# Down projection of a cross-attention and quantised FFN layer: a ring of four residual buffers in place of two, and two staging tiles

## The reference

```python
def _act_fake_quant(x, clip_factor):
    scale = jax.nn.sigmoid(clip_factor) * jnp.max(jnp.abs(x)) / QMAX
    return jnp.clip(_ste_round(x / scale), -QMAX - 1.0, QMAX) * scale
...
x = x + attention(layernorm(x), ctx)          # below: x1
xq = _act_fake_quant(layernorm(x), clip_x[0])
gate = xq @ quant(w_gate).T                   # 512 -> 1408
up = xq @ quant(w_up).T
h = _act_fake_quant(silu(gate) * up, clip_down[0])
x = x + h @ quant(w_down).T                   # 1408 -> 512
```

## Time and profile before

| | us |
|---|---|
| runs shown (3), median | 1185.84 (1184.47 to 1187.43) |
| the profiled execution, its time | 1187.88 |
| its span, first to last instruction | 1186.0 |
| PE busy | 1106.8 (93%) |
| DVE busy | 802.1 (68%) |
| ACT busy | 619.7 (52%) |
| POOL busy | 401.5 (34%) |

### The profile page before, as it was taken

The page is one execution under the profiler, slowest core; times in us unless marked ns, Lnnn a source line. Parts: engine busy times, 40 slices in busy tenths (PEclk is TensorE's granted clock), DMA queues, the critical chain, the costliest instruction groups (busy, mean ns, idle before and its releaser), DMA issues. The chain is left out here.

```text
span 1186.0 us, 17468 instructions
## 1 busy us (share of the span) xinstructions
PE 1106.8 (93%) x6173; PEld 625.7 (53%) x6202; DVE 802.1 (68%) x1478; ACT 619.7 (52%) x757; POOL 401.5 (34%) x317
## 2 busy tenths in 40 slices
PE   5988999999999999999999969999999999699898
PEld 4645555655666666666665534444444444244333
DVE  5455667677766776766655567787777777566565
ACT  3346555454555555554544436657566664754450
POOL 5454444355353644343321200000000000357578
PEclk8979999999999999999999979999999999799999
DMA  6234556556454545443215626766767512799977
GB/s 238 69 89 110 157 149 160 150 160 152 146 152 143 166 129 164 130 142 104 75 54 161 223 75 230 250 223 234 241 220 253 171 52 89 320 413 418 422 298 261
DMA packets 138736, 219.23 MB, mean 185 GB/s; under 512 B 59040, under 2 KB 67872, under 8 KB 132768
## 3 DMA queue, kind: packets, MB, share of 16 engines
q1 hardware_dynamic: 138656, 218.19, 56.3%
HBM read 133.48 MB, written 72.48 MB: 174 GB/s over the span
## 5 line engine op out<-in xcount | busy, mean ns | idle before, releaser
L1038 POOL TENSOR_TENSOR c_y<-x,c_y 128x512 f32<-128x512 f32 x64 | 112.7, 1794 | 395.2 <-DVE c_y L1072 380.5
L690 PE MATMUL a_Q<-a_xT,wq 128*128 128x512 f32 x768 | 199.8, 410 | 19.0 <-POOL a_xT L425 16.8
L690 PEld LDWEIGHTS a_Q<-a_xT,wq 128*128 128x128 f32 x768 | 144.2, 194 | 73.4 <-issue 22.6
L960 PE MATMUL e_G<-e_cT,gu 128*128 128x512 bf16 x689 | 180.0, 381 | 2.3 <-ACT e_cT L883 1.5
L924 DVE SCALAR_TENSOR_TENSOR h<-e_U,x_gus,e_sg 128x512 f32<-128x512 f32 x176 | 131.8, 749 | 73.2 <-PE e_U L964 47.4
L869 ACT ACTIVATE e_sg<-e_G,x_gus 128x512 f32<-128x512 f32 x176 | 119.0, 685 | 117.6 <-PE e_G L960 117.6
L964 PE MATMUL e_U<-e_cT,gu 128*128 128x512 bf16 x690 | 179.7, 381 | 0.7
L735 PE MATMUL a_O<-a_wo,a_aT 128*128 128x512 f32 x720 | 176.8, 395 | 0.0
L1110 PE MATMUL c_Y<-dn,gu 128*128 128x512 bf16 x704 | 156.8, 386 | 13.5 <-DVE gu L1065 13.5
L501 ACT ACTIVATE a_qT<-a_q 128x512 fp32r<-128x512 f32 x64 | 40.4, 631 | 216.9 <-DVE a_q L599 216.9
L735 PEld LDWEIGHTS a_O<-a_wo,a_aT 128*128 128x128 f32 x720 | 133.4, 189 | 28.0 <-issue 2.5
(11 more groups left out here) (128 smaller groups left out, 1351.0 us busy)
## 6 DMA issues: line engine op xcount, KB each, us to landing
x<-x_d SPq DMA_DIRECT2D x32, 1024.0 KB, 7.4
h_d<-h SPq DMA_DIRECT2D x24, 1024.0 KB, 4.1
h<-h_d SPq DMA_DIRECT2D x11, 1536.0 KB, 17.2
a_xr<-in_x SPq DMA_DIRECT2D x64, 256.0 KB, 2.9
a_xt<-in_xT SPq DMA_DIRECT2D x64, 256.0 KB, 3.1
x_d<-a_xr SPq DMA_DIRECT2D x64, 256.0 KB, 2.0
a_xs<-in_x SPq DMA_DIRECT2D x60, 256.0 KB, 2.9
out<-c_y SPq DMA_DIRECT2D x15, 1024.0 KB, 9.7
```

Of the source, the lines that this page charges most:

```text
L690: mm = nc.tensor.matmul(Q[:], wq[:, wp, j, P * n.g:P * (n.g + 1)], xT[:, n.par, xp, j], start=(ins == 0), stop=(ins == 3 * KT - 1))
L960: mm = nc.tensor.matmul(G[:, t % GU], gu[:, t, k], cT[:, p, k], start=(k == 0), stop=(k == KT - 1))
L1038: nc.gpsimd.tensor_tensor(y[:, p, t], x1[:, p, t], y[:, p, t], ALU.add).then_inc(added, 1)
```

## The change

`contract` alone is edited.

- **x1 buffers.** The store buffer of before (2 x 4 tiles) becomes `z` and joins `x1` in a ring of four block buffers, `ring(k)`. POOL adds the scaled tile into the residual in place (L1059), and the output is stored from the ring (L1034). SP loads the x1 of blocks 2 and 3 at the very start (L1021), and of block k+1 in turn k (from 3 on), after a wait for the store of block k-3, whose buffer it takes.
- **Staging.** `y` has only two tiles. The scaling of tile i waits until POOL has added tile i-2.
- **First block.** Its 11 inner tiles are coded and cast in pieces of 1, 1, 2, 2, 2 and 3 (`FIRST_CH`); PE takes its 44 matmuls inner tile by inner tile, over four PSUM banks, as the pieces come (L1120).
- **Later blocks.** PE waits for each of the two chunks only where it reads it (L1130). All loops are written out.
- **Last block.** DVE, not POOL, adds its residual (L1093), tile by tile after the scaling.
- **The scale.** The copy to `tall` is gone; the transpose reads `tmax` broadcast, and a `memset` of one column carries the signal.

```diff
--- before.py
+++ after.py
@@ -987,61 +987,76 @@
         dns = sb("h_dns", [P, D])
         c8 = sb("c_c8", [P, 2, IT, TOK], I8)
         cb = gu[:].rearrange("p t k n -> p (t k n)").rearrange("p (b t n) -> p b t n", b=2, t=IT)
-        tall = sb("h_tall", [P, P])
-        y = sb("c_y", [P, 2, TT, D])
+        z = sb("c_z", [P, 2, TT, D])
+        y = sb("c_y", [P, 2, D])
         Y = ps("c_Y", [P, 2 * TT, D])
         s_tmax, s_gmax, s_hinv, s_own = (sem("h_" + n) for n in ("tmax", "gmax", "hinv", "own"))
         h_in = [[sem(f"c_h_in{n}{b}") for b in range(NH)] for n in range(2)]
-        x1_in = [sem(f"c_x1_in{p}") for p in range(2)]
-        y_out = [sem(f"c_y_out{p}") for p in range(2)]
-        coded, cast, downed, scaled, added = (sem("c_" + n) for n in ("coded", "cast", "downed", "scaled", "added"))
+        x1_in = [sem(f"c_x1_in{r}") for r in range(4)]
+        y_out = [sem(f"c_y_out{r}") for r in range(4)]
+        last_out = sem("c_last_out")
+        coded, cast, downed, scaled, added, last_added = (sem("c_" + n) for n in (
+            "coded", "cast", "downed", "scaled", "added", "last_added"))
         CH = ((0, 6), (6, IT))
-        LAST = BLOCKS // 2
+        FIRST_CH = ((0, 1), (1, 2), (2, 4), (4, 6), (6, 8), (8, IT))
+        LAST = BLOCKS - 1
+
+        def pieces(k):
+
+            return FIRST_CH if k == 0 else CH
+
+        def upto(k, tile):
+
+            return sum(len(pieces(b)) for b in range(k)) + sum(hi <= tile for _, hi in pieces(k))
+
+        def ring(k):
+
+            return x1[:, k % 4] if k % 4 < 2 else z[:, k % 4 - 2]
 
         with nc.Block() as block:
 
             @block.sync
             def _(sp):
                 def load_x1(k):
-                    sp.dma_start(x1[:, k % 2], x1_d[ORDER[k]].rearrange("t p d -> p t d")).then_inc(x1_in[k % 2], 16)
-
-                for k in range(BLOCKS + 2):
+                    sp.dma_start(ring(k), x1_d[ORDER[k]].rearrange("t p d -> p t d")).then_inc(x1_in[k % 4], 16)
+
+                load_x1(2)
+                load_x1(3)
+                for k in range(BLOCKS + 1):
                     if k < BLOCKS - NH:
 
-                        for n, (a, z) in enumerate(CH):
-                            sp.wait_ge(coded, k * len(CH) + n + 1)
-                            sp.dma_start(h[:, BUFFER[k], a:z].rearrange("p t n -> p (t n)"),
-                                         h_d[ORDER[k + NH], :, TOK * a:TOK * z]).then_inc(h_in[n][k % NH], 16)
+                        for n, (a, e) in enumerate(CH):
+                            sp.wait_ge(coded, upto(k, e))
+                            sp.dma_start(h[:, BUFFER[k], a:e].rearrange("p t n -> p (t n)"),
+                                         h_d[ORDER[k + NH], :, TOK * a:TOK * e]).then_inc(h_in[n][k % NH], 16)
                     if k >= 2:
-
-                        if k - 2 < BLOCKS - 1:
-                            sp.wait_ge(added, (k - 1) * TT)
-                        if k - 2 < BLOCKS - 1:
-                            sp.dma_start(out_t[ORDER[k - 2]].rearrange("t p d -> p t d"), y[:, k % 2]).then_inc(y_out[k % 2], 16)
-                        if k < BLOCKS:
-                            load_x1(k)
+                        sp.wait_ge(added, (k - 1) * TT)
+                        sp.dma_start(out_t[ORDER[k - 2]].rearrange("t p d -> p t d"), ring(k - 2)).then_inc(y_out[(k - 2) % 4], 16)
+                    if 3 <= k < LAST:
+
+                        sp.wait_ge(y_out[(k - 3) % 4], 16 * ((k - 3) // 4 + 1))
+                        load_x1(k + 1)
 
                 for t in range(TT):
-                    sp.wait_ge(added, (BLOCKS - 1) * TT + t + 1)
-                    sp.dma_start(out_t[ORDER[BLOCKS - 1], t], y[:, 1, t]).then_inc(y_out[1], 16)
-                sp.wait_ge(y_out[0], 16 * LAST)
-                sp.wait_ge(y_out[1], 16 * (LAST - 1 + TT))
+                    sp.wait_ge(last_added, t + 1)
+                    sp.dma_start(out_t[ORDER[LAST], t], ring(LAST)[:, t]).then_inc(last_out, 16)
+                for r in range(4):
+                    sp.wait_ge(y_out[r], 16 * len(range(r, LAST, 4)))
+                sp.wait_ge(last_out, 16 * TT)
+
+            def residual_in(eng, k):
+
+                if k >= 2:
+                    eng.wait_ge(x1_in[k % 4], 16 * (k // 4 + (k % 4 >= 2)))
 
             @block.gpsimd
             def _(pool):
-                def add(u, p):
-                    k = 2 * u + p
-                    if not isinstance(u, int) or u > 0:
-                        pool.wait_ge(x1_in[p], 16 * u)
+                for k in range(LAST):
+                    residual_in(pool, k)
                     for t in range(TT):
-                        pool.wait_ge(scaled, k * TT + t + 1)
-                        nc.gpsimd.tensor_tensor(y[:, p, t], x1[:, p, t], y[:, p, t], ALU.add).then_inc(added, 1)
-
-                add(0, 0)
-                add(0, 1)
-                with pool.Fori(1, LAST) as u:
-                    for p in range(2):
-                        add(u, p)
+                        i = k * TT + t
+                        pool.wait_ge(scaled, i + 1)
+                        nc.gpsimd.tensor_tensor(ring(k)[:, t], ring(k)[:, t], y[:, i % 2], ALU.add).then_inc(added, 1)
 
             @block.scalar
             def _(act):
@@ -1049,73 +1064,72 @@
                 for k in range(BLOCKS):
 
                     if k >= 2:
-                        act.wait_ge(cast, (k - 1) * len(CH))
-                    for n, (lo, hi) in enumerate(CH):
+                        act.wait_ge(cast, upto(k - 2, IT))
+                    for lo, hi in pieces(k):
                         if k >= NH:
-                            act.wait_ge(h_in[n][k % NH], 16 * (k // NH))
+                            act.wait_ge(h_in[CH.index((lo, hi))][k % NH], 16 * (k // NH))
                         nc.scalar.activation(c8[:, k % 2, lo:hi], h[:, BUFFER[k], lo:hi], ACT.Copy, scale=hinv[:, 0:1]).then_inc(coded, 1)
 
             @block.vector
             def _(dve):
-                def to_bf16(u, p):
-                    k = 2 * u + p
+                own = Chain(dve, s_own)
+
+                def to_bf16(k):
                     after(dve, downed, (k - 1) * TT, 1 << 30)
-                    for n, (lo, hi) in enumerate(CH):
-                        dve.wait_ge(coded, k * len(CH) + n + 1)
-                        nc.vector.tensor_copy(cb[:, p, lo:hi], c8[:, p, lo:hi]).then_inc(cast, 1)
-
-                def scale(u, p):
-                    k = 2 * u + p
-                    after(dve, y_out[p], 16 * u, 1 << 30)
+                    for lo, hi in pieces(k):
+                        dve.wait_ge(coded, upto(k, hi))
+                        nc.vector.tensor_copy(cb[:, k % 2, lo:hi], c8[:, k % 2, lo:hi]).then_inc(cast, 1)
+
+                def scale(k):
                     for t in range(TT):
-                        dve.wait_ge(downed, k * TT + t + 1)
-                        nc.vector.tensor_tensor(y[:, p, t], Y[:, TT * p + t], dns[:], ALU.mult).then_inc(scaled, 1)
-
-                own = Chain(dve, s_own)
+                        i = k * TT + t
+                        after(dve, added, min(i - 1, LAST * TT), 1 << 30)
+                        dve.wait_ge(downed, i + 1)
+                        nc.vector.tensor_tensor(y[:, i % 2], Y[:, TT * (k % 2) + t], dns[:], ALU.mult).then_inc(scaled, 1)
+                        if k == LAST:
+                            dve.wait_ge(scaled, i + 1)
+                            if t == 0:
+                                residual_in(dve, k)
+                            nc.vector.tensor_tensor(ring(k)[:, t], ring(k)[:, t], y[:, i % 2], ALU.add).then_inc(last_added, 1)
+                            dve.wait_ge(last_added, t + 1)
+
                 own.step(nc.vector.tensor_reduce(tmax[:], hmax[:], AX.X, ALU.max))
-                nc.vector.tensor_copy(tall[:], tmax[:].to_broadcast([P, P])).then_inc(s_tmax, 1)
+                nc.vector.memset(gmax[:], 0.0).then_inc(s_tmax, 1)
                 dve.wait_ge(s_gmax, 1)
                 own.step(nc.vector.tensor_reduce(gmax[:], Y[:, 2 * TT - 1, 0:P], AX.X, ALU.max))
                 dve.wait_ge(ds_in, 16)
                 own.step(nc.vector.tensor_scalar(sh[:], gmax[:], sig[:, 1:2], 1.0 / QMAX, ALU.mult, ALU.mult))
                 nc.vector.reciprocal(hinv[:], sh[:]).then_inc(s_hinv, 1)
                 own.step(nc.vector.tensor_scalar(dns[:], dscale[:], sh[:, 0:1], None, ALU.mult))
-                to_bf16(0, 0)
-                to_bf16(0, 1)
-                scale(0, 0)
-                to_bf16(1, 0)
-                scale(0, 1)
-                to_bf16(1, 1)
-                scale(1, 0)
-                with dve.Fori(2, LAST) as u:
-                    to_bf16(u, 0)
-                    scale(u - 1, 1)
-                    to_bf16(u, 1)
-                    scale(u, 0)
-                scale(LAST - 1, 1)
+                to_bf16(0)
+                for k in range(BLOCKS):
+                    if k < LAST:
```

(25 more changed lines are left out.)

## The result

The changed kernel took 1178.81 us in the median of four runs (1178.49 to 1180.82), the kernel before 1186.55 (1184.47 to 1187.43, four runs: the three of the table above and one more). The ratio is 0.9937, with a 95% interval of 0.9925 to 0.9949: 7.7 us less. The forecast was 1175.1 in a range of 1170.5 to 1180.0, and 10.7 us less. Sign and range held; three of the eleven microseconds did not come.

What follows compares the result with a forecast made beforehand. Before: an empty start, a full DMA queue, then a PE-set end. Span 1012.1 + 11.9 + 143.1 (15 PE blocks) + 4.2 + 4.0 = 1175.3; adjusted from profiled execution to median, 1175.1 us. Range 1170.5 to 1180.

Steps and rivals of the forecast that it cites:

- The start: Block 0: first matmul at 1012.1 instead of 1017.65, block taking 11.9 us and ending at 1024.0 instead of 1029.6.
- The worth of the start: Block 0's earlier end, counted as 5.6 us of the 10.7 us gain.
- The loop of DVE and POOL: Middle blocks: one turn of casts, scalings and additions takes 9.0 us, under PE's 9.54 us a block.
- the coupling rival: DVE and POOL's loop exceeds PE's block: mild about 1178 (chance 0.07), hard above 1189 (chance 0.05).
- The late x1: Block 11's x1 lands at 1135.9 in the full queue, so PE loses 4.2 us at blocks 12 and 13.
- the signs: Trace marks of being right: among them POOL waiting for x1 in blocks 7 to 12, PE idle only between 1125 and 1145.
- the constant of 3.7 us: Added to the queue sum for block 11's x1, for landing and what the sum lacks; taken from the kernel before.
- The end: From PE's last matmul to the end of the span: 4.0 us instead of 5.8, a gain of 1.8.
- PE bound throughout: Rival: transfers land a little sooner, the 4.2 us of late-data loss vanish, 1170.9 us; chance 0.17.
- Queue order: Rival: SP's store wait ahead of the next h load makes x1 and h 11.8 us later, 1187; 0.09 with fetch.
- instruction fetch: Rival: about 1,050 more PE instructions from written-out loops pass the full queue; put at nothing; 0.09 with queue order.

Runs made afterwards that it cites:

- both mends: Changed kernel with the next h block loaded after the turn's store and x1 from turn 5 on, and four staging tiles: 1170.62 us, ratio 0.9865.
- the run with late x1 loads: Changed kernel with the x1 of blocks 2 and 3 loaded in turns 1 and 2, behind h loads, not at the stage's start: 1182.63 us, ratio 0.9963.
- the ring alone: Changed kernel with block 0 in two chunks, x1 of blocks 2 and 3 loaded in turns 1 and 2, last block added by POOL: 1182.86 us, ratio 0.9969.

## Why the prediction was right in its range, and 3 us off

- *The start.* First matmul 2.53 us after the transpose; the sum had 1012.1 - 1009.52 = 2.6. Block 0 took 10.9 us (1011.07 to 1021.99), not 11.9, as less of it ran at the lower clock: some 3 us (0.50 from 1011, 1.00 from 1014), for some 4.5 before (1017.65 to just after 1022). The granted clock of the changed kernel, then of the kernel before:

```profile
1013.00:1014.00 1.00, 1.00 (x3) 0.29 (x2) 0.69 (x1) 1.00 (x2) 0.00 (x0) 0.51 1.04 406
1014.00:1015.00 1.00, 1.00 (x6) 0.49 (x5) 0.69 (x1) 1.00 (x2) 0.00 (x0) 1.00 1.06 401
```
```profile
1021.00:1022.00 1.00, 1.00 (x4) 0.42 (x3) 0.93 (x1) 1.00 (x2) 0.00 (x0) 0.50 1.03 440
```

  Right, and one us better than the sum.
- *The worth of the start.* The sum made the loss a difference from PE's own schedule and then called the start 5.6 us of the gain. Its own term contradicts this: with the landing of block 11's x1 given, what PE wins at the start it loses in the gap, so that by its own numbers only 5.6 - 4.2 = 1.4 us of the start were left. Three pairs of runs show it: the same edit brought nothing, or a small loss, in the kernel before and in the changed one, and 3 to 4 us with both mends, where no landing holds PE up. This was the faulty step in the reading, though not in the sum.
- *The loop of DVE and POOL.* I had 9.0 us a turn, or 9.2 to 9.3 if an addition kept DVE out for its whole length. It is 8.6 while no x1 is late: POOL starts on its blocks at 1022.87, 1031.37, 1039.94 and 1048.51. Below 9.54; the coupling rival did not happen.
- *The late x1*, the term of the sum that failed: **4.2 written, 8.0 measured**. The path from landing to PE was right: second chunk 7.9 us after POOL's start on block 11, for 8.1. The landing was not: 126.4 us after the transpose in the sum (1135.9 - 1009.52), 129.3 measured, 2.9 later. PE was 1.0 us earlier at block 0, so the gap grew by that too: 4.2 + 2.9 + 1.0 = 8.1. Of the signs, POOL was to wait in blocks 7 to 12 and PE only after 1125; it was blocks 5 to 11, and PE's first gap ends at 1109.98.
- *Why it landed later.* 1.2 of the 2.9 us are the early loads, worth 3.1 and not 4.3. Why they are worth less is open: the queue moves 300 GB/s in its first 4.7 us, but it starts slowly before the change too (269 GB/s from 1013.70 to 1018.00), and the constant of 3.7 us, read off that kernel, holds this already. The other 1.7 are there in the run with late x1 loads too (132.4 us for 4.2 + 122.8 + 3.7 = 130.7) and stay open in the main. Some 0.5 of them are a slower queue between 1031.3 and 1041.3, 385 GB/s for 406 in the kernel before (1032 to 1042). The stretch from the first load to the landing reads in the changed kernel, and then before the change,

```profile
1008.10:1137.80 129.70, 121.97 (x554) 54.04 (x555) 87.65 (x82) 76.83 (x34) 71.09 (x44) 0.99 1.01 406
```
```profile
1013.60:1137.70 124.10, 114.71 (x511) 50.69 (x512) 77.83 (x69) 69.33 (x28) 72.64 (x40) 0.95 1.02 412
```

  so 129.7 us at 406 GB/s had moved 52.7 MB, while 51.6 MB stand ahead of that x1 or are it: about 1 MB from behind it had gone first (2.5 us). Before, it is 51.1 MB for 50.6, about 0.5 MB. The constant held this half MB and not the other, which would be some 1.2 us; no run separates it.
- *The end.* 1177.1 - 1173.06 = 4.0 us after PE, for 4.0. Right. Only 0.6 of the 1.8 us is DVE's addition; with POOL adding the last block (the ring alone) the end is 4.6, as POOL was not behind any more.
- *The rivals.* PE bound throughout (0.17) was wrong for this kernel, and is the kernel with both mends, at 1170.6 for 1170.9. Queue order and instruction fetch: the order was the very term that was too small, by 3.8 and not by 11.8; after block 0 PE, in the written-out loops, shows no gap for anything but DVE's casts.

Put together, by the lengths of the stage: the ring alone 4.1 us (176.5 to 172.3), the first block coded by tiles and the last added by DVE together 0.6 (to 171.7), the early x1 loads 3.1 (to 168.6), 7.9 in all. By the medians these are 4.3, 0.2 and 3.8, each uncertain by about a us. The last block by DVE is worth 0.6 by the traces, so the first block brings nothing.

## What to carry to other kernels

In this full queue the time of an operand was its place in the queue: count the bytes ahead of the load that is wanted first. Prefetches issued in front of loads that are wanted sooner cost about what two missing staging tiles did; changing the order was worth 5.3 us, with no byte less, and the two tiles 5.7. A gain ahead of such a landing was worth nothing until the landing stopped binding, so try it again after each mend (nothing twice, then 3 to 4 us). When a gap closes, look at the end too: with four staging tiles alone, PE ran almost without a gap and the tail grew from 4.0 to 7.4 us.

## What the runs showed that I had not expected

- By the time that the x1 of block 11 had landed, about 1 MB more than its place in the queue asks for had moved (above). At the queue's rate that is some 2.5 us; that it is a reason for the late landing was worked out from two stretches and not tested.
- DVE's addition with both operands in SBUF took 0.69 us, as the scaling from PSUM, in three of four cases, but 1.02 in the first, beside POOL's last addition:

```profile
1163.50 4.94 POOL L1059 TENSOR_TENSOR c_z<-c_z,c_y 128x512 f32<-128x512 f32 x4 [2.09 <-DVE c_y L1088]
...
1167.97 1.02 DVE L1093 TENSOR_TENSOR c_z<-c_z,c_y 128x512 f32<-128x512 f32 x1
...
1173.92 0.69 DVE L1093 TENSOR_TENSOR c_z<-c_z,c_y 128x512 f32<-128x512 f32 x1
```

  POOL is busy until 1168.44, so the two overlap for 0.47 us. The Trainium skill ("SBUF — State Buffer", "Who interferes with whom") has a DVE instruction with two SBUF inputs contend with a GpSimd instruction that reads SBUF, as POOL's addition does; the row agrees, with 0.33 us more for an overlap of 0.47.
- A gap of 2.1 to 2.2 us in PE was followed by a block of 11.35 us in some cases and of 9.67 in others (in the kernel before 2.21 and 2.15). Gaps of about the same sum split in two (1.2 and 0.9, in the changed kernel) were not followed by a slow block: the granted clock reads 1.00 in all its stretches after 1018. Waiting chunk by chunk, which moves the gaps but not the end of the casts, may so save the 1.7 us of such a block; it was not tried alone.
